# Attention and mixture-of-experts layer: last weight chunks, exponentials and down weights moved between engines around the start of the expert blocks

## The chip, the cores and the metric

One core of a Trainium2 chip runs the whole kernel in a single launch. The metric is the device time of one execution in microseconds; lower is better. Engine names: PE is TensorE's matmul stream, PEld its weight loads, DVE is VectorE, ACT is ScalarE, POOL is GpSimd, SP is SyncE. Where a row has a "q" behind the engine's name, it is the engine's queue, which also issues DMAs.

## What is computed

The input is 16 sequences of 512 rows of 256 numbers. A residual layer of windowed attention with a latent branch comes first, then a residual feed-forward layer with shared weights and 8 experts, of which each row uses 2. The second layer is the part that matters here:

```python
x = x + _layernorm(attention(_layernorm(x)))
x = x + _layernorm(ffn(_layernorm(x)))

# ffn, for every row: E = 8 experts, K = 2 chosen, F = 352, shared F = 704
scores = softmax(x @ gate_w.T)
topk_w, topk_i = top_k(scores, K)
topk_w = topk_w / (topk_w.sum(-1, keepdims=True) + 1e-20) * 2.5
combine = zeros((T, E)).at[arange(T)[:, None], topk_i].set(topk_w)
g = silu(einsum('td,edf->etf', x, w_gate)) * einsum('td,edf->etf', x, w_up)
y = einsum('te,etd->td', combine, einsum('etf,efd->etd', g, w_down))
return y + (silu(x @ sw_gate) * (x @ sw_up)) @ sw_down
```

## The kernel before, in words

The program runs in four parts. The attention of all 16 sequences comes first. In the second part (lines 1968 to 2230) the router chooses the experts of all rows, and the shared feed-forward layer is computed for the first 8 sequences, in 8 steps; `m` counts them from 0 to 7. In the third part (lines 2236 to 2533) the chosen experts work through 135 blocks of 128 rows. In the fourth part the shared layer of the other 8 sequences is computed and everything is summed. There is no loop in hardware: every instruction is written out, each engine works through its own list in order, and semaphores hold the lists together.

Exact products in single precision are made of three matmuls, so every weight and every row is needed as a rounded high part and as a remainder (the raw number minus the high part). The weights of the experts are prepared while the second part runs:

- **Gate and up weights** come in 16 chunks of 128x704 (`expert_chunk`, line 1988). POOL makes the high part and the remainder of each in `split_chunk` (line 2028): a copy at line 2032 and a subtraction at line 2034. Chunks 14 and 15 are split by POOL after all its scatters. Chunk 15 has its own place in `arena`; the others pass through `chunk_in`.
- **Down weights** come as three parts, `n` = 0, 1, 2, of 128, 128 and 96 partitions by 2048. In the third part DVE rounds parts 0 and 1 and forms their remainders (lines 2398 to 2403); ACT rounds part 2 (line 2345) and DVE forms its remainder (line 2408).
- **The list of rows**: POOL scatters the number of every row into `list_scratch` with indirect DMAs (line 2025), 8 for each of two kinds of sequences in each step. In the last step DVE forms the `table` (`finish_table`, line 2101), which says for every block where its names stand and which expert it uses.

In the last step (`m` = 7) of the second part six slices `n` = 0 to 5 of the shared hidden layer pass: PE's `gate_up`, ACT's `gate_silu` (line 534), DVE's `hidden` (line 551), ACT's `hidden_high` (line 540), DVE's `hidden_low` (line 557), PE's `shared_down`. ACT does `first_chunk(n)`, which is `gate_silu` of slice n and then `hidden_high` of slice n. `h_used` counts PE's finished `shared_down`.

At the start of the third part:

- **SP** waits for the table and for the landing of all scatters (`lists_written`), and then loads names in groups (`GROUPS`, line 2236). Group n waits until group n - 3 has landed. The last shared result is stored behind group 2.
- **POOL** waits for `h_used` and then gathers the rows of a block (`gather`, line 2293, DMA at line 2300), which needs the names' group. Six gathers run ahead; then gather b + 6 alternates with scatter b.
- **PE** does 18 matmuls whose result nobody reads (line 2457), then waits for the table, for all chunks and for ACT's reading of the shared result. Then `turn_rows` of blocks 0 and 1 (line 2472), and in step b: `block_gate_up` b (lines 2484 to 2486, 12 matmuls), `turn_rows` b + 2, `turn_hidden` b - 1 (line 2494), `down` b - 2 (lines 2505 to 2507). Before step 2 it waits for the remainders of all three parts of the down weights:

```python
for b in range(NBLK + 2):
    if b == 2:
        pe.wait_ge(down_low, FCE)
```

- **ACT** first makes the exponentials for the router's weights (line 2319) and a small Silu that brings the other function table back (line 2320), rounds part 2 and then works on the blocks (`rows_high` at 2324, `gate` at 2330).
- **DVE** works on the down weights and then on the blocks: `rows_low` (line 2371), `gated_hidden` (line 2376), `hidden_low` (lines 2380 and 2382).

## Time and profile before

| what | value |
|---|---|
| three runs | 1854.68, 1858.62 and 1861.70 us, median 1858.62 |
| the profiled execution's own time | 1857.21 us |
| its span in the profile | 1855.3 us |
| mean granted clock of TensorE over the span | 0.978 of full speed |
| busy share of PE, PEld, DVE, ACT, POOL | 94%, 77%, 68%, 53%, 50% |
| third part (the expert blocks), from the trace | about 1132 to 1632 us |

The span is what lies between the first and the last instruction of the trace; the execution's own time is 1.9 us longer. A row of a timeline gives the start in microseconds from the span's beginning, the duration, the engine and line of the code, what is written and read, and in brackets how long the engine had been idle before and what released it. A row of windows gives, for a stretch A:B, its length, the busy time of each engine asked for, the granted clock of TensorE as a share of its full 2.4 GHz (1.00 is 2.4 GHz, 0.50 is 1.2 GHz), the mean busy share of the DMA engines and the GB/s they moved.

### The profile page before, as it was taken

To read this page: it belongs to the slowest core of one execution; us is meant where nothing else is said; L and a number is where in the kernel's file an instruction comes from. 1 tells how busy PE (TensorE), PEld (TensorE's weight loads), DVE (VectorE), ACT (ScalarE), POOL (GpSimd) and SP (SyncE) were. 2 spreads that over 40 slices of the span, in tenths; PEclk is the share of its full clock that TensorE was granted. 3 is DMA by queue.
4 is the path that set the end of the run, shared out by engine and by line. 5 is a ranking of instruction groups with operands and counts; after the bars stand their busy time and mean duration, and the time that the engine had idled before them with its cause. 6 is when DMAs were issued, how large, how long until landed. Compare 5 with 4: busy or idle time off the path is not lost.

```text
span 1855.3 us, 39544 instructions
## 1 busy us (share of the span) xinstructions
PE 1740.7 (94%) x13060; PEld 1425.3 (77%) x13060; DVE 1259.0 (68%) x3077; ACT 992.1 (53%) x2309; POOL 932.3 (50%) x1117
## 2 busy tenths in 40 slices
PE   4999999999999999997999998999999999989996
PEld 3566666666666666655888887999999999978886
DVE  7778888888888888785776775433333333358787
ACT  2566666777777667666333333444444444435554
POOL 3445555555555555554378766455555555401101
PEclk8999999999999999998999999999999999999999
DMA  6655556655565665443254322233222222257875
GB/s 120 100 74 92 103 102 127 115 98 102 103 101 100 109 115 104 92 91 120 92 113 89 90 42 57 70 76 87 75 75 75 75 75 76 71 191 184 204 210 97
DMA packets 164113, 189.78 MB, mean 102 GB/s; under 512 B 41777, under 2 KB 121970, under 8 KB 163922
## 3 DMA queue, kind: packets, MB, share of 16 engines
q1 hardware_dynamic: 136642, 142.92, 36.9%
q0 software_dynamic: 24976, 43.41, 9.4%
q8 instruction: 116, 1.90, 0.5%
q10 hardware_dynamic: 2304, 0.93, 0.3%
q14 instruction: 75, 0.61, 0.2%
HBM read 84.87 MB, written 51.40 MB: 73 GB/s over the span
## 4 chain that ended last, share of the span: by engine, by line
PE 69%; DVE 8%; ACT 7%; issue 6%; POOL 5%; SPq 3%; DMA 1%; ACTq 1%; POOLq 0%; DVEq 0%
PE bank L496 5%; PE bank L497 5%; PE bank L498 5%; PE bank L1636 5%; PE bank L2485 4%; PE bank L2486 4%; PE bank L2484 4%; PE bank L1693 4%; PE bank L1658 4%; PE bank L1638 3%; ACT prob L1074 3%; PE bank L1637 3%; PE bank L2505 2%; PE bank L2506 2%; PE bank L2507 2%
## 5 line engine op out<-in xcount | busy, mean ns | idle before, releaser
L924 POOL TENSOR_SCALAR_AFFINE_SELECT prob<-prob 128x512 f32<-128x512 f32 x256 | 162.9, 636 | 380.3 <-ACT prob L1074 380.2
L1074 ACT ACTIVATE prob<-bank 128x512 f32<-128x512 f32 (+1 forms) x512 | 249.0, 539 | 103.4 <-PE bank L1680 100.8
L2376 DVE TENSOR_TENSOR b_h<-b_h,bank 128x352 f32<-128x352 f32 x135 | 70.4, 521 | 287.3 <-ACT b_h L2330 287.3
L2306 POOL DMA_INDIRECT y_scratch<-b_y,names x135 | 133.6, 989 | 176.4 <-ACT b_y L2341 172.4
L1399 DVE COPY_PREDICATED bank<-from_prev,bank 128x512 f32<-128x512 int32 x192 | 133.1, 693 | 96.2 <-PE bank L1658 92.0
L1402 DVE TENSOR_REDUCE row_max<-bank 128x4 f32<-128x512 f32 x256 | 177.3, 693 | 25.8 <-PE bank L1658 18.5
L2484 PE MATMUL bank<-wgu_h,bxT_h 128*128 x540 | 176.5, 327 | 0.0
L2485 PE MATMUL bank<-wgu_l,bxT_h 128*128 x540 | 176.2, 326 | 0.0
L2330 ACT ACTIVATE b_h<-bank 128x352 f32<-128x352 f32 x135 | 62.7, 464 | 211.9 <-PE bank L2486 211.9
L2486 PE MATMUL bank<-wgu_h,bxT_l 128*128 x540 | 175.3, 325 | 0.0
L2300 POOL DMA_INDIRECT bx<-xn_scratch,names x135 | 134.6, 997 | 54.6 <-issue 39.2
L1693 PE MATMUL bank<-prob,v_sb 128*32 128x256 f32 (+1 forms) x2048 | 159.4, 366 | 0.0
L2025 POOL DMA_INDIRECT list_scratch<-names,pos x128 | 128.3, 1002 | 46.9 <-issue 36.1
L1658 PEld LDWEIGHTS bank<-kS,qS 48*128 48x128 f32 x1024 | 78.3, 189 | 92.9 <-issue 48.7
L1658 PE MATMUL bank<-kS,qS 48*128 48x256 f32 (+1 forms) x1024 | 127.8, 328 | 20.9 <-DVE row_max L1402 20.8
L928 POOL TENSOR_SCALAR_AFFINE_SELECT prob<-prob 128x512 f32<-128x512 f32 x192 | 128.3, 668 | 0.0
L2505 PE MATMUL bank<-wd_h,bhT_h 128*128 (+1 forms) x405 | 125.5, 310 | 0.7 <-ACT b_y L2341 0.7
L2507 PE MATMUL bank<-wd_h,bhT_l 128*128 (+1 forms) x405 | 114.7, 283 | 0.0
L2506 PE MATMUL bank<-wd_l,bhT_h 128*128 (+1 forms) x405 | 114.2, 282 | 0.0
L2634 POOL DMA_DIRECT2D out_dram<-f_ys x15 | 19.5, 1300 | 186.9 <-ACT f_ys L2656 186.9
L1680 PE MATMUL bank<-qS,kS 49*128 49x256 f32 (+1 forms) x1024 | 106.6, 285 | 5.3 <-ACT prob L1074 4.6
L2485 PEld LDWEIGHTS bank<-wgu_l,bxT_h 128*128 128x128 f32 x540 | 102.7, 190 | 0.0
(359 smaller groups left out, 5247.5 us busy)
## 6 DMA issues: line engine op xcount, KB each, us to landing
kS<-qk_h SPq DMA_DIRECT2D x128, 128.0 KB, 3.9
qS<-qk_h SPq DMA_DIRECT2D x128, 128.0 KB, 5.8
f_y<-y_scratch SPq DMA_DIRECT2D x16, 1024.0 KB, 9.2
x_in<-in_L_attn_x_dram SPq DMA_DIRECT2D x16, 512.0 KB, 6.2
kS<-qk_l SPq DMA_DIRECT2D x64, 128.0 KB, 4.8
qS<-qk_l SPq DMA_DIRECT2D x64, 128.0 KB, 6.6
x_res<-in_L_attn_x_dram SPq DMA_DIRECT2D x16, 512.0 KB, 4.1
out_dram<-x_res SPq DMA_DIRECT2D x16, 512.0 KB, 5.1
```

Of the source, the lines that this page charges most:

```text
L924: op = e.affine_select(out=own, in_=own, compare_op=ALU.is_gt, fill=0.0, base=0, pattern=[[0, HG], [1, P]], channel_multiplier=-1)
L1074: e.activation(prob[:, u % SLOTS, 2 * hp:2 * hp + 2, 0:w], src[:, :, 0:w], ACT.Exp, scale=SCALE).then_inc(keyed.frees[hp], 1)
L1402: e.tensor_reduce(row_max[:, g, :, b], own, AX.X, ALU.max).then_inc(score_free, 1)
L1658: op = e.matmul(SB[:, par, hh * WIN + lo:(hh + 1) * WIN], qS[rows, buf, tile, b * P:(b + 1) * P], kS[rows, buf, tile, k0:k0 + w], start=(b ...
L1693: op = e.matmul(PV[h * PAD:(h + 1) * PAD, b * P:b * P + w], v_sb[:, buf, b, g * HG + h, :], prob[:, u % SLOTS, 2 * (h % 2) + h // 2, 0:w], ...
L2300: e.indirect_dma_start(out=bx[:, b % 4, :], out_offset=None, in_=rows_dram, in_offset=bass.IndirectOffsetOnAxis(ap=b_names[:, b, 0:1], axis=0)
L2484: e.matmul(out_, xh, wh, start=(c == 0), stop=False)
L2485: e.matmul(out_, xh, wl, start=False, stop=False)
L2486: op = e.matmul(out_, xl, wh, start=False, stop=(c == C - 1))
L2505: e.matmul(out_, hh, wh, start=(n == 0), stop=False)
L2506: e.matmul(out_, hh, wl, start=False, stop=False)
L2507: op = e.matmul(out_, hl, wh, start=False, stop=(n == FCE - 1))
```

## The change

Five things are edited, all around the border of the second and the third part.

1. POOL no longer splits chunks 14 and 15. ACT makes their high parts in the last step, after slices 1 and 2, and waits there until chunk 15 has landed. DVE makes the remainders, chunk 14's behind `experts_reached` and chunk 15's behind `hidden_low` of slice 3.
2. The exponentials move on ACT from the start of the third part into the last step, behind slice 3. The small Silu is left out.
3. ACT rounds all three parts of the down weights, part 0 ahead of the copy of the last shared result, parts 1 and 2 behind it. That copy moves from the second part to the third. DVE only forms the remainders: part 0 first, part 1 behind `rows_low` of blocks 0 and 1, part 2 behind its step 0 of the blocks.
4. Names are loaded in groups of 1, 1, 2, 4, 8, 16, 32 and 71 blocks, not 1, 1, 2, 12, 40 and 79.
5. PE's matmuls that nobody reads are 14, not 18. The buffer `b_h` lies behind `bhT_h` and `bhT_l`, not ahead of them, and ACT's wait for the stored shared result moves from `gate` to `hidden_turned`.

```diff
-            ROUTE_STEPS, END_STEPS, WEIGHT_STEPS, LAST_STEPS = 20, 8, 12, 17
+            ROUTE_STEPS, END_STEPS, WEIGHT_STEPS, LAST_STEPS = 20, 8, 10, 17
...
-        b_h = sb("b_h", [P, 2, F])
         bhT_h = sb("bhT_h", [P, 2, FCE, P], f32r)
         bhT_l = sb("bhT_l", [P, 2, FCE, P], f32r)
+        b_h = sb("b_h", [P, 2, F])
...
                     for kind in "ba":
                         scatter(kind, HALF - 1)
-                    for k in (CHUNKS - 2, CHUNKS - 1):
-                        split_chunk(k)
...
+                    def last_chunk_high(k):
+
+                        act.wait_ge(stage_in, 32 * CHUNKS)
+                        act.wait_ge(stage_split, CHUNKS - 2)
+                        nc.scalar.activation(parts_of(k)[0], chunk_of(k), ACT.Copy).then_inc(chunk_high, 1)
+
+                    def exponentials():
+
+                        act.wait_ge(member_ready, 2 * HALF)
+                        nc.scalar.activation(probs, lg_all[:, :, :], ACT.Exp).then_inc(exp_ready, 1)
...
+                            if m == HALF - 1:
+                                if n in (1, 2):
+                                    last_chunk_high(CHUNKS - 3 + n)
+                                if n == 3:
+                                    exponentials()
                         if m + 1 < HALF:
                             gate_silu(act, m + 1, 0, h_f)
-                    result(HALF - 1)
...
+                    def last_chunk_low(k):
+
+                        dve.wait_ge(chunk_high, k + 1)
+                        hi, lo = parts_of(k)
+                        e.tensor_tensor(lo, chunk_of(k), hi.bitcast(f32), ALU.subtract).then_inc(stage_split, 1)
...
                         experts_reached()
+                        last_chunk_low(CHUNKS - 2)
                         hidden(dve, m, 3, h_f)
                         hidden_low(dve, m, 3, h_f, h_h, h_l)
+                        last_chunk_low(CHUNKS - 1)
                         finish_table()
...
-            GROUPS = [range(0, 1), range(1, 2), range(2, 4), range(4, 16), range(16, 56), range(56, NBLK)]
+            GROUPS = [range(0, 1), range(1, 2), range(2, 4), range(4, 8), range(8, 16), range(16, 32), range(32, 64), range(64, NBLK)]
...
-                    act.wait_ge(member_ready, 2 * HALF)
-                    e.activation(probs, lg_all[:, :, :], ACT.Exp)
-                    e.activation(picked[:, 0:1, :], lg_all[:, 0:1, :], ACT.Silu).then_inc(exp_ready, 1)
...
                     act.wait_ge(down_in, 16 * FCE)
+                    act.wait_ge(table_ready, 1)
+                    down_rounded(0)
+                    act.wait_ge(h_used, FCS * HALF)
+                    for n in range(2):
+                        shared_result(act, HALF - 1, n, lambda n: y_sb[:, 2 * n:2 * n + 2, :].rearrange("p t d -> p (t d)"))
+                    act.wait_ge(stage_split, CHUNKS)
+                    down_rounded(1)
                     act.wait_ge(hl_ready, FCS * HALF)
-                    e.activation(wd_h[0:fe[LATE], LATE, :, :], wd_f[0:fe[LATE], LATE, :, :], ACT.Copy).then_inc(down_high, 1)
+                    down_rounded(2)
                     rows_high(0, 0)
                     rows_high(1, 1)
...
-                    dve.wait_ge(down_in, 16 * FCE)
-                    for n in range(LATE):
+                    def down_remainder(n):
+                        dve.wait_ge(down_high, n + 1)
                         hi, lo, raw_ = down_part(n)
-                        if n == 1:
-                            dve.wait_ge(stage_split, CHUNKS)
-                        link(e.tensor_copy(hi, raw_))
                         e.tensor_tensor(lo, raw_, hi.bitcast(f32), ALU.subtract).then_inc(down_low, 1)
+
+                    down_remainder(0)
                     rows_low(0, 0)
                     rows_low(1, 1)
-                    dve.wait_ge(down_high, 1)
-                    hi, lo, raw_ = down_part(LATE)
-                    e.tensor_tensor(lo, raw_, hi.bitcast(f32), ALU.subtract).then_inc(down_low, 1)
+                    down_remainder(1)
...
                         step(b, b % 2)
+                        if b == 0:
+                            down_remainder(2)
...
-                    for _ in range(18):
+                    for _ in range(14):
                         e.matmul(psum[0][:, :], wsd_h[:, 0, 0:P], ws_h[:, 0, 0:4 * P], start=True, stop=True)
```

On ACT, from the Silu of slice 4 of the last step to the first blocks, this stood in a row before (`h_f` and `h_h` are the slices, `rows_a` written from `lg_all` holds the exponentials, `y_sb` the shared result, `wd_h` the rounded down weights, `bxT_h` the turned rows of a block):

```order
L534 ACTIVATE h_f<-bank 128x512
L540 ACTIVATE h_h<-h_f 128x512
L534 ACTIVATE h_f<-bank 64x512
L540 ACTIVATE h_h<-h_f 64x512
L544 ACTIVATE y_sb<-bank 128x512 x2
L2315 UNCONDITIONAL_BRANCH
L2319 ACT_TABLE_LOAD
L2319 ACTIVATE rows_a<-lg_all 128x512
L2320 ACT_TABLE_LOAD
L2320 ACTIVATE rows_a<-lg_all 128x8
L2345 ACTIVATE wd_h<-wd_l 96x2048
L2324 ACTIVATE bxT_h<-bank 128x256 x2
```

With the change ACT's list from the high part of slice 2 on reads:

```order
L540 ACTIVATE h_h<-h_f 128x512
L2071 ACT_TABLE_LOAD
L2071 ACTIVATE rows_a<-lg_all 128x512
L534 ACT_TABLE_LOAD
L534 ACTIVATE h_f<-bank 128x512
L540 ACTIVATE h_h<-h_f 128x512
L534 ACTIVATE h_f<-bank 64x512
L540 ACTIVATE h_h<-h_f 64x512
L2338 UNCONDITIONAL_BRANCH
L2363 ACTIVATE wd_h<-wd_l 128x2048
L544 ACTIVATE y_sb<-bank 128x512 x2
L2363 ACTIVATE wd_h<-wd_l 128x2048
```

The two table loads now stand ahead of `gate_silu` of slice 4, and behind the last slice one rounding stands ahead of the shared result and two behind it.

On DVE, at the start of the third part (`wd_l` is the remainder of the down weights, `b_h` the hidden rows of a block), this stood before:

```order
L2402 CAST wd_h<-wd_l 128x2048
L2403 TENSOR_TENSOR wd_l<-wd_l,wd_h 128x2048
L2402 CAST wd_h<-wd_l 128x2048
L2403 TENSOR_TENSOR wd_l<-wd_l,wd_h 128x2048
L2371 TENSOR_TENSOR bxT_l<-bank,bxT_h 128x256 x2
L2408 TENSOR_TENSOR wd_l<-wd_l,wd_h 96x2048
L2376 TENSOR_TENSOR b_h<-b_h,bank 128x352
L2371 TENSOR_TENSOR bxT_l<-bank,bxT_h 128x256
```

With the change:

```order
L2429 TENSOR_TENSOR wd_l<-wd_l,wd_h 128x2048
L2400 TENSOR_TENSOR bxT_l<-bank,bxT_h 128x256 x2
L2429 TENSOR_TENSOR wd_l<-wd_l,wd_h 128x2048
L2405 TENSOR_TENSOR b_h<-b_h,bank 128x352
L2400 TENSOR_TENSOR bxT_l<-bank,bxT_h 128x256
L2429 TENSOR_TENSOR wd_l<-wd_l,wd_h 96x2048
L2405 TENSOR_TENSOR b_h<-b_h,bank 128x352
```

Both copies are gone from DVE, and the remainders of parts 1 and 2 have moved back behind the first work on blocks.

## Rows read from the trace of the kernel before

**Rows 1.** The page: busy time, share of the span and instructions

```profile
PE 1740.7 (94%) x13060; PEld 1425.3 (77%) x13060; DVE 1259.0 (68%) x3077; ACT 992.1 (53%) x2309; POOL 932.3 (50%) x1117
```

**Rows 2.** Timeline of PE around the border, start, duration, instruction, idle before

```profile
1118.57 0.40 PE L496 MATMUL bank<-rT_h,ws_h 128*128 128x512 f32 x1
...
1132.14 4.27 PE L2457 MATMUL bank<-ws_h,wsd_h 128*128 128x512 f32 x18
1139.55 0.44 PE L2472 MATMUL bank<-ident,bx 128*128 128x128 f32 x2 [3.15 <-DMA bx<-xn_scratch,names]
1142.61 0.69 PE L2472 MATMUL bank<-ident,bx 128*128 128x128 f32 x2 [2.62 <-DMA bx<-xn_scratch,names]
1142.95 0.64 PE L2484 MATMUL bank<-wgu_h,bxT_h 128*128 x1
...
1149.71 0.41 PE L2484 MATMUL bank<-wgu_h,bxT_h 128*128 x1
...
1153.77 0.33 PE L2484 MATMUL bank<-wgu_h,bxT_h 128*128 x1
...
1157.32 0.33 PE L2484 MATMUL bank<-wgu_h,bxT_h 128*128 x1
```

**Rows 3.** The chain of waits, from the last scatter to the first names

```profile
1126.61 4.62 DMA list_scratch<-names,pos
1131.46 2.55 DMA names<-list_scratch
```

**Rows 4.** Timeline of POOL: a scatter of the list, gathers 0, 1 and 4

```profile
1119.74 1.48 POOL L2025 DMA_INDIRECT list_scratch<-names,pos  x1 [0.30 <-issue]
...
1134.81 2.90 POOL L2300 DMA_INDIRECT bx<-xn_scratch,names  x1 [0.50 <-issue]
1138.01 2.73 POOL L2300 DMA_INDIRECT bx<-xn_scratch,names  x1 [0.30 <-issue]
...
1149.08 0.95 POOL L2300 DMA_INDIRECT bx<-xn_scratch,names  x1 [5.84 <-DMA names<-list_scratch]
```

**Rows 5.** Timeline of DVE in the last step and behind it

```profile
1119.68 0.69 DVE L557 TENSOR_TENSOR h_l<-h_f,h_h 128x512 fp32r<-128x512 f32 x1 [0.70 <-ACT h_h L540]
...
1125.79 0.67 DVE L551 TENSOR_TENSOR h_f<-h_f,bank 128x512 f32<-128x512 f32 x1
1127.15 1.76 DVE L557 TENSOR_TENSOR h_l<-h_f,h_h 128x512 fp32r<-128x512 f32 x1 [0.70 <-ACT h_h L540]
...
1132.77 3.68 DVE L2403 TENSOR_TENSOR wd_l<-wd_l,wd_h 128x2048 fp32r<-128x2048 f32 x1
...
1137.62 2.29 DVE L2403 TENSOR_TENSOR wd_l<-wd_l,wd_h 128x2048 fp32r<-128x2048 f32 x1
...
1143.75 0.42 DVE L2371 TENSOR_TENSOR bxT_l<-bank,bxT_h 128x256 fp32r<-128x256 f32 x1 [2.88 <-ACT bxT_h L2324]
```

**Rows 6.** Timeline of SP: the names of blocks 4 to 15

```profile
1134.77 12.69 SPq L2275 DMA_DIRECT2D names<-list_scratch  x12
```

**Rows 7.** Timeline of ACT in the last step and behind it

```profile
1112.40 0.63 ACT L540 ACTIVATE h_h<-h_f 128x512 fp32r<-128x512 f32 x1 [2.67 <-DVE h_f L551]
...
1133.50 1.28 ACT L2319 ACT_TABLE_LOAD   x1
1134.80 0.64 ACT L2319 ACTIVATE rows_a<-lg_all 128x512 f32<-128x512 f32 x1
...
1136.85 1.89 ACT L2345 ACTIVATE wd_h<-wd_l 96x2048 fp32r<-96x2048 f32 x1
```

**Rows 8.** Windows: length, clock, DMA share and GB/s, where chunk 15 has landed

```profile
1114.50:1114.75 0.25, 1.00 0.01 1
```

**Rows 9.** Windows: length, PE busy, clock, DMA share and GB/s

```profile
1143.60:1146.60 3.00, 3.00 (x11) 0.50 0.25 50
...
1147.60:1149.20 1.60, 1.60 (x11) 0.99 0.25 63
```

**Rows 10.** Line 2025: time from issue to landing of all 128 scatters

```profile
DMA to landing us min/median/max: 2.5/4.3/7.4
```

More of the change, by code:

```diff
@@ L1978, in chunk_of, with parts_of @@
                     return chunk_in[:, :] if k < CHUNKS - 1 else arena[:, LAST_CHUNK:LAST_CHUNK + 2 * F]
+                def parts_of(k):
+                    return tuple(w[:, k, :, :].rearrange("p k f -> p (k f)") for w in (wgu_h, wgu_l))
                 def store_result(sp, m):
@@ L2028, in split_chunk @@
                     def split_chunk(k):
-                        hi, lo = (w[:, k, :, :].rearrange("p k f -> p (k f)") for w in (wgu_h, wgu_l))
-                        gp.wait_ge(stage_in, 32 * (CHUNKS if k >= CHUNKS - 2 else k + 1))
+                        hi, lo = parts_of(k)
+                        gp.wait_ge(stage_in, 32 * (k + 1))
                         e.tensor_copy(hi, chunk_of(k)).then_inc(chunk_high, 1)
@@ L2326, in gate @@
                     def gate(b, u):
-                        if isinstance(b, int) and b == 0:
-                            act.wait_ge(ys_stored, 16 * HALF)
                         act.wait_ge(bg_full, b + 1)
@@ L2341, in result, with down_rounded @@
                         e.activation(b_y[:, u, :], psum[5][:, 0:D], ACT.Copy).then_inc(by_read, 1)
+                    def down_rounded(n):
+                        e.activation(wd_h[0:fe[n], n, :, :], wd_f[0:fe[n], n, :, :], ACT.Copy).then_inc(down_high, 1)
                     act.wait_ge(down_in, 16 * FCE)
+                    act.wait_ge(table_ready, 1)
[5 more added lines that the diff above has]
+                    down_rounded(1)
                     act.wait_ge(hl_ready, FCS * HALF)
-                    e.activation(wd_h[0:fe[LATE], LATE, :, :], wd_f[0:fe[LATE], LATE, :, :], ACT.Copy).then_inc(down_high, 1)
+                    down_rounded(2)
                     rows_high(0, 0)
```

4 lines of the change are left out of this document (3 added, 1 removed).

## The prediction

> **What bounds the kernel now.** I read the page first: PE is busy for 94% of the span, no other engine over 77% [rows 1], so time is to be had only where PE stands still or is slow. The change touches nothing but the border between the shared layer and the expert blocks, so I read PE's timeline there. The reader is to see two holes behind the 18 unread matmuls: 3.15 us until the rows of block 0 are there and 2.62 us until those of block 1 are [rows 2]. Then PE is slow: eleven matmuls in 3.00 us at 1143.6 to 1146.6, with a granted clock of 0.50 (1.2 GHz), after PE had been idle for 3.15 us, busy for 0.44 and idle again for 2.62; from 1147.6 on it is eleven in 1.60 at 0.99 [rows 2, 9]. From block 2 to block 3 PE needs 4.06 us (1149.71 to 1153.77), from 3 to 4 it needs 3.55 (to 1157.32) [rows 2]. After that the blocks follow at 3.55 us, and nothing in the change alters that pace. So the question is how much earlier block 3 begins.
>
> What holds the rows back is a chain [rows 3, 4]: the last scatter is issued at 1126.61 and lands 4.62 us later, SP issues the first names at 1131.46, they land 2.55 us later at 1134.0, and POOL gathers. POOL was busy with chunk 15 until 1134.31 and begins at 1134.81, only 0.8 us late. But its two gathers take 2.90 and 2.73 us, where the later one takes 0.95 [rows 4]. PE's two turns start 1.84 and 1.87 us after these gathers' ends.
>
> Why were they slow? DVE's subtraction of 2.29 us starts at 1137.62 and ends at 1139.91; gather 1, begun inside it at 1138.01, ends 0.83 us after that [rows 4, 5]. The scatter begun at 1119.74, inside a DVE subtraction that ends at 1120.37, takes 1.48 us and ends 0.85 after it [rows 4, 5]. And DVE's subtraction begun at 1132.77, while POOL subtracts for chunk 15 until 1134.31, takes 3.68 us, not 2.29 [rows 5]: POOL and DVE hold each other up while both read this memory.
>
> **Part by part.**
>
> *Chunks 14 and 15 leave POOL.* POOL is free from 1127.6. It gains the 0.8 us until the names' landing, no more, as SP's chain is not shortened. `hidden_low` of slice 4, which took 1.76 us beside POOL's work, takes 0.69 [rows 5]; that brings PE's end of the shared layer from 1132.14 to about 1131.1, ahead of the names, so it is worth nothing by itself.
>
> *ACT takes the high parts.* ACT is free at 1113.03 [rows 7], but chunk 15 lands only at about 1114.5, where the DMA share falls to 0.01 [rows 8]: a wait of 1.5 us. Behind it in ACT's queue stands `gate_silu` of slice 2. The copy of 704 numbers I put at 0.79 us, between 0.63 for 512 and 1.89 for 2048 [rows 7]. Slice 2's Silu (0.6) then ends at 1115.9 and DVE has read the banks at 1116.6, some 1.3 us later than before. PE asks for these banks again at 1118.57, for slice 4 [rows 2]. Cost on the path: zero, as long as chunk 15 lands before about 1116.4.
>
> *DVE takes the remainders.* Each is 0.89 us by the rate of 0.69 for 512 and 2.29 for 2048 [rows 5]. DVE had idle time before the table, so these cost DVE nothing on the path. They can cost POOL: the scatters start every 1.27 us, and one that starts inside a remainder waits. Bounds: zero if both fall between starts, 2 x 0.89 = 1.8 us if both hit at once. The one hit of 0.5 us before [rows 4] moves as well. I reckon starts against my shifted DVE times and find one hit and the old one gone or shifted: 0.3 us later names.
>
> *The exponentials.* Two table loads of 1.28 us and 0.64 us of work [rows 7] now stand ahead of slice 4's Silu. ACT had the high part of slice 3 at 1119.68 [rows 5]; the late slice 2 (1.3) and chunk 14's remainder (0.89) make that at most 1121.9, and 1121.5 by my reckoning, as DVE was idle for 0.3 in between. So Silu ends at 1121.5 + 1.28 + 0.64 + 1.28 + 0.6 = 1125.3. DVE wants it behind the table, at 1125.79 [rows 5]: hidden, with 0.5 us to spare. The rows show no pause around a load: it begins at 1133.50 and the exponential starts at 1134.80, 1.30 us later [rows 7]. The Trainium skill ("ScalarE: Activation LUTs", What ACT_TABLE_LOAD costs) speaks against this step: it counts a drain of about 1380 ns beside each load's 1283. This trace does not show it. By that page Silu would end 2.8 us later, 2.2 after DVE wants it, and the whole gain below would fall from 4.9 to 3.7 us, as an estimate; I go by the rows.
>
> *Down weights.* ACT had slice 5's high part at 1130.3 (DVE's 0.69 us and PE's last eight matmuls lie between it and 1132.14), and has it 1.1 earlier now, at 1129.2. It rounds part 0 in 1.89 us [rows 7] to 1131.1, copies the shared result to 1132.4 and rounds two parts to 1136.2. It is wanted for block 0's rows at 1137.6, so this is hidden by 1.4 us. DVE's remainder of part 0 then lies at 1131.1 to 1133.4, over before the first gather. That is the core of the gain: gathers 0 and 1 meet no DVE subtraction. The Trainium skill ("SBUF — State Buffer", Who interferes with whom) says that a VectorE instruction with two inputs in this memory and a GpSimd instruction that reads it shut each other out for a whole instruction. The trace agrees for those begun inside (0.83 and 0.85 us after the end). By that rule the remainders of parts 1 and 2 would hold gathers 4 and 5, which I find harmless below.
>
> *Start of the blocks, by the rows.* Names land at 1134.0 + 0.3 = 1134.3. Gather 0 runs to 1135.3 (0.95 us), gather 1 starts 0.30 us later and ends at 1136.55. PE turns block 1 at + 1.87 = 1138.4 and starts block 0's matmuls 0.34 later [rows 2], at 1138.8: **4.2 us** before 1142.95. The clock: PE's unread matmuls now end at about 1131.1 + 14 x 0.237 = 1134.4, then 2.7 us idle and 0.9 us idle. Before, idle of 3.15 and 2.6 brought it down; I take full clock, since the second hole is short. Block 0's twelve matmuls then take 2.0 us. DVE's low part of block 1 comes 1.14 us after PE's turn [rows 2, 5], at 1139.55 to 1139.9; the remainder of part 1 runs until 1142.2, the hidden rows of block 0 (0.45) and the low part of block 2 (0.35) until 1143.0, and part 2's remainder until 1145.3. PE would be ready for block 2 at 1143.7, but waits for that remainder: a **new stall of 1.6 us**. Block 2 starts at 1145.35, 4.36 us before 1149.71 [rows 2].
>
> *Names in growing groups.* Gather 4 waited 5.84 us for twelve names that SP issued at 1.06 us each [rows 4, 6]. Four names now need 4.2 us and land at about 1140.8; gathers 4 and 5, even held up to the ends of both remainders, land at 1145 and 1148.5, ahead of PE's need at 1147.4 and 1151. Later groups stay ahead: SP issues a name in 1.06 us, a block lasts 3.55. So block 3 follows in 3.55 us, not 4.06: **0.5 us**. Buffer places and moved waits: nothing.
>
> **Sum:** 4.2 + 0.16 + 0.5 = 4.9 us. Against the profiled execution's 1857.21 us that is 1852.3; the median of the runs shown is 1.4 us above that execution, and against it the sum gives **1853.7 us**.
>
> **The bounds.** Clock low in block 0: its matmuls take 3.5 us, but most hides in the new stall, and 0.5 is lost; low through block 2 as well, 2.0 more. Scatters hit: between + 0.3 and - 1.5. No stall at block 2: + 1.6. The last scatter's landing: 4.62 us here, but 2.5 at least and 7.4 at most over all [rows 10], so + 2.1 or - 2.8. ACT and DVE copies at half speed beside others: see below.
>
> **The rivals.**
> - *Larger gain.* POOL's splitting delayed the last landing, and it falls towards 2.5 us: names 2.1 us earlier, 1858.6 - 7.0 = **1851.6**. For it: POOL worked on chunks just then. Against: the median landing is 4.3 anyway.
> - *The gain comes back at block 2.* DVE's remainders of parts 1 and 2 take 3.68 us each, as beside POOL before [rows 5]. Block 2 starts 2.8 us later than above, leaving 2.1: **1856.5**. For it: gathers 4 and 5 run just then. Against: a gather is short, the subtraction that took 3.68 met POOL's own long one.
> - *The table loads cost more than the rows show,* or the change moves a wait rather than removing it: slice 4 is 2.2 us late, part 0's remainder runs until 1135.6 and holds gather 0 by 1.15: **1854.9**.
> - *Slower than before.* If ACT's first rounding is late enough that part 0's remainder lies over gathers 0 and 1, they take 2.90 and 2.73 us again, block 0 starts at 1142.95 as before, and now two remainders of up to 3.68 us stand between block 1's low part and block 2, where before part 2's alone stood: 1144.1 + 3.7 + 0.4 + 0.4 + 3.7 = 1152.3, 2.6 us after 1149.71; less the 0.5 of the names: **1860.7**. It decides from the point where ACT ends the rounding of part 0 more than 1.0 us later than I reckon. For it: DVE has no slack at block 2. Against: ACT's row of 1.89 us has no contention in it.
>
> **How the numbers follow.** Forecast 58%, larger gain 14%, given back at block 2 12%, table loads 8%, slower 8%. About 0.5%, or 9.3 us, is what a measurement of this kernel can tell from no change. None of the cases reaches that by itself: faster by more needs every favourable bound together (2.1 + 1.6 on top of 4.9) and a favourable median, 9%; slower by more 4%; within it 87%. The three runs shown lie 3.9 us below to 3.1 above their median, so the range is 1848.5 to 1859.5; it holds all cases but the slowest, with the spread of a median.
>
> **What would show it.** Right: gathers 0 and 1 under 1.1 us; block 0's first matmul near 1138.8 and block 3's near 1148.9; PE waiting 1 to 2 us at block 2 for DVE's remainder; ACT idle about 1.5 us ahead of the first chunk copy; Silu of slice 4 done before 1125.8. Wrong: long gathers again, a first turn later than 1139, PE waiting for slices in the last step, a clock of 0.50 beyond block 1, or a difference that lies outside 1110 to 1160 us.

## The result, and the profile after

The changed kernel runs in 1849.26 us in the median of 14 runs (1841.80 to 1853.67); the kernel before, timed beside it, in 1858.01 us (1850.71 to 1865.91, 14 runs). The ratio is 0.995, with an interval from 0.9935 to 0.9965: 8.75 us faster by the medians, where 4.9 were forecast. The time lies in the range of the prediction, 0.8 us above its lower end, but the gain is 1.8 times the sum. The profiled execution took 1851.47 us.

The page of the changed kernel, span and busy times:

```profile
span 1849.7 us, 39539 instructions
PE 1739.9 (94%) x13056; PEld 1424.9 (77%) x13056; DVE 1252.8 (68%) x3077; ACT 996.1 (54%) x2312; POOL 926.4 (50%) x1113
```

The span is 5.6 us shorter than before [rows 1]. It has to be divided, because this execution was slower in a part that the change does not touch. ACT's first table load of the second part, before and after:

```profile
875.08 1.28 ACT L534 ACT_TABLE_LOAD   x1
```

```profile
877.13 1.28 ACT L534 ACT_TABLE_LOAD   x1
```

And POOL's first scatter of the last 16, before and after:

```profile
1106.90 0.97 POOL L2025 DMA_INDIRECT list_scratch<-names,pos  x1 [2.22 <-DVE pos L700]
```

```profile
1110.53 0.96 POOL L2028 DMA_INDIRECT list_scratch<-names,pos  x1 [2.22 <-DVE pos L700]
```

The changed kernel came 3.63 us later to this scatter, from where both do the same work. From there to the end of the span it gained 5.6 + 3.6 = 9.2 us. In the fourteen profiles of this study the table load begins anywhere from 869.0 to 877.1 us, though no instruction ahead of it differs. These 8.1 us are two thirds of the 11.9 us over which the changed kernel's 14 runs spread. So for every kernel I use a **stretch** that this does not touch: from the first of the last 16 scatters to the start of ACT's Silu of block 20. It is 114.38 us before (1106.90 to 1221.28) and 105.28 us after (1110.53 to 1215.81): 9.10 us, which agrees with the 8.75 of the medians. Behind it nothing differs: 634.0 us to the end of the span before, 633.9 after.

Every stretch is read from one execution, and it holds some chance as well. In ten kernels gather 0 waits for nothing but its names and still begins at places up to 0.66 us apart: 26.96 us behind the first scatter in `e4_dve_rounds`, 27.62 in `e12_all_three`; in an eleventh, `e6_unread25`, at 28.52. So a difference of less than about 0.7 us between two stretches is not shown by the stretches alone, and I say where gather 0 began when it matters.

Times behind the first scatter are written with a plus: before, block 0's first matmul starts at +36.05. PE around the border, after, answering to [rows 2]:

```profile
1134.68 3.36 PE L2485 MATMUL bank<-ws_h,wsd_h 128*128 128x512 f32 x14
1140.88 0.44 PE L2500 MATMUL bank<-ident,bx 128*128 128x128 f32 x2 [2.83 <-DMA bx<-xn_scratch,names]
1142.00 0.44 PE L2500 MATMUL bank<-ident,bx 128*128 128x128 f32 x2 [0.69 <-DMA bx<-xn_scratch,names]
1142.35 0.42 PE L2512 MATMUL bank<-wgu_h,bxT_h 128*128 x1
...
1149.62 0.42 PE L2512 MATMUL bank<-wgu_h,bxT_h 128*128 x1 [0.80 <-DVE wd_l L2429]
...
1153.27 0.33 PE L2512 MATMUL bank<-wgu_h,bxT_h 128*128 x1
```

Block 0 starts at +31.82, 4.2 us earlier than before; block 2 at +39.09, behind a new wait of 0.80 us for DVE's remainder; block 3 at +42.74, 4.1 us earlier. POOL and DVE, after, answering to [rows 4, 5]:

```profile
1137.90 1.00 POOL L2323 DMA_INDIRECT bx<-xn_scratch,names  x1 [6.59 <-DMA names<-list_scratch]
1139.20 0.96 POOL L2323 DMA_INDIRECT bx<-xn_scratch,names  x1 [0.30 <-issue]
...
1143.85 2.50 POOL L2323 DMA_INDIRECT bx<-xn_scratch,names  x1 [1.17 <-DMA names<-list_scratch]
```

```profile
1134.83 2.29 DVE L2429 TENSOR_TENSOR wd_l<-wd_l,wd_h 128x2048 fp32r<-128x2048 f32 x1 [1.25 <-ACT wd_h L2363]
...
1143.24 2.28 DVE L2429 TENSOR_TENSOR wd_l<-wd_l,wd_h 128x2048 fp32r<-128x2048 f32 x1
...
1147.18 2.28 DVE L2429 TENSOR_TENSOR wd_l<-wd_l,wd_h 96x2048 fp32r<-96x2048 f32 x1
```

The first two gathers take 1.00 and 0.96 us, not 2.90 and 2.73. Gather 4, begun inside the remainder of part 1 (1143.24 to 1145.52), takes 2.50 us and ends 0.83 us behind it; nobody waits for it. ACT in the last step, after, answering to [rows 7]:

```profile
1118.48 0.79 ACT L2066 ACTIVATE wgu_h<-chunk_in 128x704 fp32r<-128x704 f32 x1 [1.82 <-DMA arena<-in_L_ffn_w_up_dram]
...
1125.14 1.28 ACT L2071 ACT_TABLE_LOAD   x1
1126.43 0.63 ACT L2071 ACTIVATE rows_a<-lg_all 128x512 f32<-128x512 f32 x1
1127.09 1.28 ACT L534 ACT_TABLE_LOAD   x1
1128.38 0.60 ACT L534 ACTIVATE h_f<-bank 128x512 f32<-128x512 f32 x1
```

And a window inside block 0's matmuls: length, PE busy, clock, DMA share and GB/s. The clock is down, as in [rows 9]:

```profile
1142.80:1145.80 3.00, 3.00 (x12) 0.50 0.69 212
```

That leaves 9.1 - 4.1 = 5.0 us. My sum ended at block 5. ACT's Silu of blocks 14 and 15, before:

```profile
1194.98 0.46 ACT L2330 ACTIVATE b_h<-bank 128x352 f32<-128x352 f32 x1 [1.55 <-PE bank L2486]
...
1203.53 0.46 ACT L2330 ACTIVATE b_h<-bank 128x352 f32<-128x352 f32 x1 [2.23 <-PE bank L2486]
```

After, the same two:

```profile
1194.49 0.46 ACT L2347 ACTIVATE b_h<-bank 128x352 f32<-128x352 f32 x1 [1.55 <-PE bank L2514]
...
1198.04 0.46 ACT L2347 ACTIVATE b_h<-bank 128x352 f32<-128x352 f32 x1 [1.55 <-PE bank L2514]
```

Between these blocks 8.55 us passed before, and 3.55 do now. What stopped it before, on POOL and then on PE:

```profile
1195.38 0.97 POOL L2300 DMA_INDIRECT bx<-xn_scratch,names  x1 [7.79 <-DMA names<-list_scratch]
```

```profile
1198.18 0.44 PE L2472 MATMUL bank<-ident,bx 128*128 128x128 f32 x2 [3.24 <-DMA bx<-xn_scratch,names]
```

POOL stood 7.79 us with gather 16 waiting for names, and PE 3.24 us for these rows. The other 1.8 us are the clock, for the most part: it was 0.64 in the 3 us from 1198 on and 0.79 in the 3 us behind them, about 1.6 us of lost time by the busy time of PE there (2.81 x 0.36 + 3.00 x 0.21, an estimate). The list of what ended the idle time ahead of POOL's gathers (line 2300) had it in one row:

```profile
  DMA names<-list_scratch: 13.6, 2
```

Two waits, 13.6 us in all. I had accounted for one of 5.84.

### The profile page after: what moved, and what is told of

It is laid out like the page before. It is cut to its first block, busy times and chain, and to the rows that moved or that the text cites. A ratio compares the mean times of both kernels' runs of the same rounds, so it can differ in the third digit from the quotient of the medians.

```text
span 1849.7 us, 39539 instructions
## 1 busy us (share of the span) xinstructions
PE 1739.9 (94%) x13056; PEld 1424.9 (77%) x13056; DVE 1252.8 (68%) x3077; ACT 996.1 (54%) x2312; POOL 926.4 (50%) x1113
## 4 chain that ended last, share of the span: by engine, by line
PE 72%; DVE 8%; ACT 7%; issue 6%; POOL 5%; DMA 1%; ACTq 1%; SPq 0%; POOLq 0%; DVEq 0%
PE bank L496 5%; PE bank L497 5%; PE bank L498 5%; PE bank L1636 5%; PE bank L2514 5%; PE bank L2512 5%; PE bank L2513 5%; PE bank L1693 4%; PE bank L1658 4%; PE bank L1638 4%; PE bank L1637 4%; ACT prob L1074 3%; PE bank L2533 3%; PE bank L2534 3%; PE bank L2535 3%
## 5 line engine op out<-in xcount | busy, mean ns | idle before, releaser
L2512 PEld LDWEIGHTS bank<-wgu_h,bxT_h 128*128 128x128 f32 x540 | 101.9, 189 | 1.2 <-issue 1.1
```

What stands on the lines that cost most here:

```text
L2512: e.matmul(out_, xh, wh, start=(c == 0), stop=False)
```

## The experiments

My theory A after the result: more than half of the gain is the growing groups. The old group of 40 names, issued by SP at 1.06 us each, landed too late for block 16. The rival, theory B, is my prediction's own split: 0.5 us for the groups, the rest from work moved between engines.

### Groups alone, and everything but the groups

`e1_groups_only`, on the kernel before:

```diff
-            GROUPS = [range(0, 1), range(1, 2), range(2, 4), range(4, 16), range(16, 56), range(56, NBLK)]
+            GROUPS = [range(0, 1), range(1, 2), range(2, 4), range(4, 8), range(8, 16), range(16, 32), range(32, 64), range(64, NBLK)]
```

> The kernel before with one edit: the names are loaded in groups of 1, 1, 2, 4, 8, 16, 32, 71. Measure: the stretch from the first of the last 16 scatters of the list to ACT's Silu of block 20, 114.4 us before and 105.3 us with the whole change. Theory A (the growing groups bring more than half of the gain, because block 16 no longer waits for a group of 40 names, where blocks 15 and 16 lay 8.55 us apart and not 3.55): both pauses go, 5.0 + 0.4 us, so the stretch is 109.0 us and the time about 1852.5 us. Theory B (the groups are worth the 0.5 us at block 4 that I predicted, and the rest came from the work moved between engines): 113.9 us and 1857.5 us.

Measured: stretch 109.51 us, median 1854.04 us against 1857.08 beside it (ratio 0.9991, 0.9971 to 1.001). The gap of 8.55 us is 3.55. Theory A had 109.0 and B 113.9: A holds. The timed runs alone would not show it: their interval holds no change as well as 4.9 us, and its middle is 1.7 us. The trace does, by a pause of 5.0 us that is gone. All of the gain lies there; block 3's Silu comes at +49.10, where it came at +49.00 before. The gathers stayed long:

```profile
1135.14 3.25 POOL L2300 DMA_INDIRECT bx<-xn_scratch,names  x1 [0.15 <-issue]
1138.70 2.73 POOL L2300 DMA_INDIRECT bx<-xn_scratch,names  x1 [0.30 <-issue]
```

`e2_all_but_groups`, on the changed kernel, is the same diff the other way round.

> The changed kernel with one edit undone: groups of 1, 1, 2, 12, 40, 79 again. Same stretch (114.4 before, 105.3 with the whole change). Theory A: the names of block 16 land when SP has issued 40 of them, at 1.06 us each, from a start that the change moves by only 0.1 us; what the blocks start earlier is given back at block 16: 114.2 us, blocks 15 and 16 some 12 to 13 us apart (8.55 plus the 4 us of earlier start), and a time of about 1858 us. Theory B (the parts add up): the 3.7 us that the start is earlier stay: 110.3 us, about 1854 us.

Measured: stretch 112.27 us, median 1855.06 us (ratio 1.0, 0.9986 to 1.0014). It lies between the two theories, 2.1 us better than before, 7.0 worse than the changed kernel. Block 0 starts at +31.74, as early as in the changed kernel. Then POOL and ACT show:

```profile
1143.91 0.95 POOL L2323 DMA_INDIRECT bx<-xn_scratch,names  x1 [10.32 <-DMA names<-list_scratch]
```

```profile
1142.98 0.46 ACT L2347 ACTIVATE b_h<-bank 128x352 f32<-128x352 f32 x1 [2.40 <-PE bank L2514]
...
1152.31 0.47 ACT L2347 ACTIVATE b_h<-bank 128x352 f32<-128x352 f32 x1 [2.19 <-PE bank L2514]
```

Gather 4 begins at +42.18, as in the kernel before (+42.18 there too), since the names of its group land no earlier. So the early start is given back at block 3 (9.33 us behind block 2, not 3.55), and more than that: PE stands still for 4.02 us, the clock falls behind it (0.67 from 1149 to 1152), and block 3's Silu comes at +50.58, 1.6 us later than in the kernel before. The 2.1 us are therefore not what is left of the early start. They arise at block 16, where the gap is 4.85 us and not 8.55: the blocks come 1.6 us later and the names 0.6 us earlier (gather 16 at +87.91, not +88.48), PE waits 1.08 us and not 3.24, and the clock stays at 1.00 behind so short a wait, where it was 0.64 before. I had put the place of the loss at block 16; the mechanism is the one of theory A, the place is the first group that is too large. The parts do not add: the groups are worth 4.9 us without the rest and 7.0 us with it, the rest 2.1 us without the groups and 4.2 with them.

### POOL's splitting and DVE's rounding

`e3_pool_splits`, on the changed kernel (ACT's and DVE's parts for the two chunks taken out):

```diff
                     for kind in "ba":
                         scatter(kind, HALF - 1)
+                    for k in (CHUNKS - 2, CHUNKS - 1):
+                        split_chunk(k)
...
-                                if n in (1, 2):
-                                    last_chunk_high(CHUNKS - 3 + n)
...
-                        last_chunk_low(CHUNKS - 2)
...
-                        last_chunk_low(CHUNKS - 1)
```

> The changed kernel, but POOL splits chunks 14 and 15 after its scatters as before, and ACT and DVE do nothing for them in the last step. Same stretch. Theory A (POOL and DVE shut each other out): DVE's remainder of part 0 is held until POOL's last subtraction ends, then holds gather 0 until 0.83 us after its own end; both gathers end 2.0 us later than in the changed kernel, stretch 107.4 us. Rival (POOL's splitting was hidden behind the landing of the names but for 0.5 us): gathers 0 and 1 take 0.97 us each and the stretch is 105.8 us.

Measured: stretch 106.01 us, median 1850.09 us (ratio 0.9965, 0.9943 to 0.9987). It is nearer to the rival. Gather 0 and DVE's first remainder:

```profile
1131.97 2.28 POOL L2321 DMA_INDIRECT bx<-xn_scratch,names  x1 [0.75 <-DMA names<-list_scratch]
```

```profile
1130.04 3.33 DVE L2428 TENSOR_TENSOR wd_l<-wd_l,wd_h 128x2048 fp32r<-128x2048 f32 x1 [1.24 <-ACT wd_h L2361]
```

The chain of theory A is there: DVE's remainder takes 3.33 us beside POOL, and gather 0 takes 2.28 us and ends 0.88 us behind it. But it costs 1.2 us and not 2.0, and gather 1 takes 0.95. Part of it goes into the wait at block 2, which is 0.43 us here and not 0.80, and 0.7 us are left.

`e4_dve_rounds`, on the changed kernel:

```diff
-                    act.wait_ge(table_ready, 1)
-                    down_rounded(0)
...
-                    act.wait_ge(stage_split, CHUNKS)
-                    down_rounded(1)
...
+                            link(e.tensor_copy(hi, raw_))
...
                     down_remainder(0)
+                    down_remainder(1)
                     rows_low(0, 0)
                     rows_low(1, 1)
-                    down_remainder(1)
+                    down_remainder(2)
...
-                        if b == 0:
-                            down_remainder(2)
```

> The changed kernel, but DVE rounds parts 0 and 1 of the down weights itself again and forms their remainders right away; ACT rounds part 2 and DVE forms its remainder behind the low parts of blocks 0 and 1. Same stretch. Theory A: DVE is busy on these four until about 2.8 us after the first names have landed, gather 0 takes about 3.5 us, gather 1 0.97; block 0 starts 2.5 us later than in the changed kernel, the pause of 0.8 us at block 2 goes: stretch 107.0 us. Rival (the long gathers came from POOL's own state after the splitting, not from DVE): both gathers 0.97 us, no pause at block 2, stretch 104.5 us.

Measured: stretch 105.17 us, median 1848.53 us (ratio 0.9962, 0.9945 to 0.9979): no loss that can be told. Its names came early by chance (gather 0 at +26.96, where it is +27.37 in the changed kernel), so up to 0.3 us of loss may be hidden. POOL's first two gathers:

```profile
1132.18 1.67 POOL L2323 DMA_INDIRECT bx<-xn_scratch,names  x1 [6.18 <-DMA names<-list_scratch]
1134.15 1.98 POOL L2323 DMA_INDIRECT bx<-xn_scratch,names  x1 [0.30 <-issue]
```

They are 1.67 and 1.98 us long, so DVE holds them, which the rival denies; block 0 starts 1.3 us later. Theory A's mechanism holds and its 2.5 us do not: without POOL beside it, DVE does its first copy and remainder in 1.23 and 2.29 us, not 1.68 and 3.68. And what block 0 loses comes back at block 2, where no remainder is waited for. So undoing one of the two costs 0.7 or -0.1 us, both about as small as chance, and yet `e1_groups_only`, which has both undone, is 4.2 us longer than the changed kernel.

`e9_pool_and_dve` undoes both in the changed kernel (the two diffs above together).

> The changed kernel with both undone: POOL splits chunks 14 and 15 after its scatters, and DVE rounds parts 0 and 1 of the down weights. The exponentials stay in the last step, there are 14 unread matmuls, and the growing groups stay. One of the two undone gave 106.0 and 105.2 us where the changed kernel has 105.3. Theory A (the two only cost together: POOL's last subtraction holds DVE's first, and so DVE's row of four lies over both gathers): gathers 0 and 1 about 2.9 and 2.7 us, stretch 109 us. Rival (each part has its own price, so they add; the 4.2 us that the groups alone leave come from the exponentials or from 18 unread matmuls): 105.9 us and gather 1 at 0.96 us.

Measured: stretch 109.70 us, time 1851.20 us in one execution. POOL's gathers and DVE's first remainder:

```profile
1132.12 3.10 POOL L2321 DMA_INDIRECT bx<-xn_scratch,names  x1 [0.30 <-issue]
1135.53 2.73 POOL L2321 DMA_INDIRECT bx<-xn_scratch,names  x1 [0.31 <-issue]
```

```profile
1130.28 3.69 DVE L2431 TENSOR_TENSOR wd_l<-wd_l,wd_h 128x2048 fp32r<-128x2048 f32 x1
```

Neither undone 105.28, one 106.01, the other 105.17, both 109.70: the price lies in the pair. POOL's splitting holds DVE three times: `hidden_low` of slice 4 takes 1.77 us where it takes 0.69 in `e4_dve_rounds`, the first copy 1.68 and not 1.23, the first remainder 3.69 and not 2.29. These 2.9 us make the row of four on DVE end late enough to lie over both gathers (3.10 and 2.73 us). Either edit breaks it: from 109.70 us, one alone brings 3.7 us (to 106.01) and the other alone 4.5 (to 105.17). As this kernel has the exponentials in the last step, 14 unread matmuls and the new place of `b_h` with the moved wait, and is as slow as `e1_groups_only` to within 0.2 us, those make up nothing of the 4.2 us that can be told.

### The exponentials

`e5_exp_back`, on the changed kernel:

```diff
-                                if n == 3:
-                                    exponentials()
...
+                    act.wait_ge(member_ready, 2 * HALF)
+                    e.activation(probs, lg_all[:, :, :], ACT.Exp)
+                    e.activation(picked[:, 0:1, :], lg_all[:, 0:1, :], ACT.Silu).then_inc(exp_ready, 1)
                     act.wait_ge(down_in, 16 * FCE)
                     act.wait_ge(table_ready, 1)
                     down_rounded(0)
```

> The changed kernel, but the exponentials and the small Silu stand at the start of the third part again, ahead of ACT's rounding of part 0. Stretch from the first of the last 16 scatters to the Silu of block 20: 105.3 us in the changed kernel. Theory A (ACT's queue is what feeds DVE there): 3.4 us ahead of the rounding push DVE's remainder of part 0 over gather 1, which then ends 0.8 us after it, block 0 starts 1.6 us later and, as part of that is given back in the pause at block 2, the stretch is 106.3 us. Rival (ACT has slack, the step is worth nothing): 105.3 us. If the Silu of slice 4 had been late in the changed kernel, this one would have a shorter last step; by its trace it was not.

Measured: stretch 106.62 us, time 1848.20 us in one execution. Theory A (106.3 us), with gather 1 at 1.94 us, ending 0.83 us behind the remainder; block 0 starts 1.2 us later, where 1.6 were expected. Having the exponentials early (and 14 unread matmuls, not 18) is worth nothing that can be told before ACT has the roundings (`e9_pool_and_dve` against `e1_groups_only`: 109.70 and 109.51). Once ACT has them, the early exponentials are worth 1.3 us: they make room for the roundings.

### The clock, and the wait at block 2

`e6_unread25`, on the changed kernel:

```diff
-                    for _ in range(14):
+                    for _ in range(25):
```

> The changed kernel with 25 unread matmuls, not 14, so that PE is busy until the rows of block 0 have nearly landed. Theory A (the clock falls because PE stands still for 2.8 us before block 0): the clock stays at 1.00, block 0's Silu comes 1.4 us earlier, but DVE's remainder of part 2 now decides when block 2 starts, so only half is kept: stretch 104.5 us, pause at block 2 about 1.6 us and not 0.8. Rival (the clock falls for another reason, as it did with 18 and with 14): block 0 as slow as before and 105.3 us.

Measured: stretch 105.46 us, time 1852.85 us in one execution. The clock stayed up: from block 0's first matmul to its Silu 2.24 us pass, not 3.56. But SP's first four names took 3.45 us to issue here, not 1.91, and gather 0 began 1.15 us later. Why is open. And PE waited 1.33 us for DVE's remainder at block 2, not 0.80 (1.6 expected). The late names and that longer wait cancel what the clock gave, so the run shows the clock's part and not its worth.

`e7_early_round`, on the changed kernel:

```diff
                             if m == HALF - 1:
+                                if n == 1:
+                                    act.wait_ge(down_in, 16 * FCE)
+                                    nc.scalar.activation(wd_h[:, 0, :, :], wd_f[:, 0, :, :], ACT.Copy).then_inc(down_high, 1)
...
-                    down_rounded(0)
+                    act.wait_ge(stage_split, CHUNKS)
+                    down_rounded(1)
                     act.wait_ge(h_used, FCS * HALF)
...
-                    act.wait_ge(stage_split, CHUNKS)
-                    down_rounded(1)
...
                     down_remainder(0)
+                    down_remainder(1)
                     rows_low(0, 0)
                     rows_low(1, 1)
-                    down_remainder(1)
+                    down_remainder(2)
...
-                        if b == 0:
-                            down_remainder(2)
```

> The changed kernel, but ACT rounds part 0 of the down weights in the last step while it waits for chunk 15, and part 1 at the start of the third part; DVE forms both remainders there in a row, and part 2's behind the low parts of blocks 0 and 1. Theory A (part 2's remainder is what block 2 waits for): the pause of 0.8 us at block 2 goes, gather 0 is held by about 0.1 us, block 0 starts as in the changed kernel: stretch 104.2 us. Rival (DVE's second remainder runs into the gathers and costs what it saves): gather 0 over 2 us and a stretch of 105.3 us or more.

Measured: stretch 104.18 us, median 1849.07 us (ratio 0.9965, 0.9946 to 0.9985). Theory A (104.2), closer than one execution can show: no wait at block 2, gather 0 at 1.17 us, block 0 at +31.80. The 1.1 us can be seen in the stretch alone; the timed runs do not tell this kernel from the changed one.

`e8_early_round_unread25` has both edits.

> Both edits of the two kernels before: early rounding of part 0 and 25 unread matmuls. Theory A: with the pause at block 2 gone the higher clock is kept whole, so the parts together bring more than their sum: stretch 102.7 us, about 2.6 us less than the changed kernel and 11.7 less than before, a time of about 1845.5 us where before has 1857. Rival (the parts only add: 0.8 and 1.1): 103.4 us.

Measured: stretch 103.44 us, the shortest of the study, median 1845.82 us (ratio 0.9942, 0.9922 to 0.9962). Gather 0 began at +27.00, 0.37 us earlier than in the changed kernel, so that much of it may be chance. That is the rival's number, but not by its reason: the clock is up (2.24 us to the Silu), but PE turned blocks 0 and 1 together, at +31.13, 0.8 us later than in `e7_early_round`:

```profile
1138.95 0.89 PE L2501 MATMUL bank<-ident,bx 128*128 128x128 f32 x4 [1.13 <-DMA bx<-xn_scratch,names]
```

Three more kernels went after that. `e10_early_round_unread21` has `range(21)`:

> Early rounding of part 0, and 21 unread matmuls. With 25, the turns of blocks 0 and 1 started together at 31.1 us behind the first scatter, 0.8 us later than with 14, and block 0 lost part of what the clock gave. Theory A (25 are so many that PE or its memory reads come in the way of block 0's first turn; 21 end 1 us earlier): turn at 30.3 us, clock at 1.00, stretch 102.6 us. Rival (the late turn had another cause, such as the stored shared result whose 512 KB are under way when the first rows are gathered): turn at 31 us again in this kernel, stretch 103.4 us.

Measured: stretch 104.43 us, longer than either theory has it, median 1847.13 us (ratio 0.9949, 0.9932 to 0.9967). The first turn starts at +30.58, 1.85 us behind the end of gather 0, with the store where it was; so the store does not explain the late turn in `e8_early_round_unread25` (2.69 us behind). Nor do 25 unread matmuls by themselves: `e6_unread25` has both, and its first turn starts 2.04 us behind the end of gather 0. The cause is open. The clock stays up, but a new wait appears: gather 4 began inside DVE's remainder, took 2.82 us, and PE waited for it:

```profile
1142.77 0.44 PE L2501 MATMUL bank<-ident,bx 128*128 128x128 f32 x2 [1.18 <-DMA bx<-xn_scratch,names]
```

`e11_store_later`, on `e10_early_round_unread21`:

```diff
-                        if n == 2:
-                            store_result(sp, HALF - 1)
                         if n == 3:
+                            store_result(sp, HALF - 1)
```

> The kernel with early rounding and 21 unread matmuls, and SP stores the last shared result behind the names of blocks 4 to 7, not ahead of them, so that no large transfer is under way when the rows of blocks 0 and 1 are gathered. If the store delays the first rows, PE's turn of block 0 starts 1.85 us behind the end of gather 0 and the stretch is 102.5 us, whatever the kernel without this edit does. Rival (the store costs nothing there): the same stretch as that kernel; if ACT's wait for the store then comes late, block 0's turned hidden rows wait and the stretch is longer by up to 1 us.

Measured: stretch 104.16 us, median 1848.03 us (ratio 0.9952, 0.9933 to 0.997). The first turn starts at +30.26, 1.83 us behind the end of gather 0, as in the kernel without this edit (1.85): the rival holds, the store costs nothing there. Gather 4 begins ahead of DVE's remainder (1142.89 against 1142.98) and takes 0.95 us. But the clock fell in block 0. Two windows inside block 0's matmuls, first of `e10_early_round_unread21`, then of this kernel:

```profile
1137.00:1139.00 2.00, 2.00 (x13) 1.00 0.58 148
```

```profile
1141.80:1144.80 3.00, 3.00 (x13) 0.62 0.95 290
```

`e12_all_three` is `e11_store_later` with `range(25)`:

> Early rounding of part 0, the store behind the names of blocks 4 to 7, and 25 unread matmuls. With 21 and the late store the clock fell in block 0 although PE had been idle for only 1.17 and 0.91 us ahead of it, with 21 and the early store it stayed up after 1.20 and 0.87 us, but gather 4 was held by DVE's remainder and PE waited 1.2 us for it. Theory A (with more unread matmuls the idle time ahead of the first turn is short enough, and with the late store gather 4 begins ahead of DVE's remainder and takes 0.95 us): clock at 1.00 in block 0, no pause up to block 20, stretch 102.7 us. Rival (whether the clock falls is not set by these holes alone): block 0 slow again and 104.2 us.

Measured: stretch 103.91 us, between theory A and its rival, median 1847.16 us (ratio 0.9948, 0.9929 to 0.9967). The clock stayed up, as in theory A. But SP's first names were late by 0.5 us behind the first scatter (+24.91, not +24.44), gather 4 fell into DVE's remainder again and took 2.75 us, and PE waited for it:

```profile
1143.95 0.44 PE L2500 MATMUL bank<-ident,bx 128*128 128x128 f32 x2 [0.63 <-DMA bx<-xn_scratch,names]
```

All stretches and ratios (ratio to the kernel before, timed beside each):

| kernel | stretch us | ratio | interval |
|---|---|---|---|
| before | 114.38 | | |
| everything but the groups | 112.27 | 1.0 | 0.9986 to 1.0014 |
| POOL splits, DVE rounds | 109.70 | | |
| groups alone | 109.51 | 0.9991 | 0.9971 to 1.001 |
| exponentials back | 106.62 | | |
| POOL splits | 106.01 | 0.9965 | 0.9943 to 0.9987 |
| 25 unread | 105.46 | | |
| the change | 105.28 | 0.995 | 0.9935 to 0.9965 |
| DVE rounds | 105.17 | 0.9962 | 0.9945 to 0.9979 |
| early rounding, 21 unread | 104.43 | 0.9949 | 0.9932 to 0.9967 |
| early rounding | 104.18 | 0.9965 | 0.9946 to 0.9985 |
| the same, 21 unread, later store | 104.16 | 0.9952 | 0.9933 to 0.997 |
| the same, 25 unread, later store | 103.91 | 0.9948 | 0.9929 to 0.9967 |
| early rounding, 25 unread | 103.44 | 0.9942 | 0.9922 to 0.9962 |

The kernels without a ratio were timed in one execution. No version beats the change by more than its interval. Early rounding with 25 unread matmuls has the lowest median and the shortest stretch.

## Why the prediction was right and where it failed

**The range was met by luck.** The time of 1849.26 us lies in a range of 11 us whose width came from the rivals and from the spread of three runs. The sum gave 1853.7, and 5.0 of the 9.1 us of gain lie where nothing was forecast. One of the prediction's own signs of being wrong came true: a difference outside 1110 to 1160 us, the one at blocks 14 to 16.

**Start of the blocks: right.** Names were forecast 0.3 us later behind the scatters, they came 0.1 earlier (+24.44, not +24.56). Shifted by 3.63 us, gather 0 was forecast at 1134.3 and began at 1134.27; block 0's first matmul at 1138.8 came at 1138.72; ACT waited 1.82 us for chunk 15 (forecast 1.5); the Silu of slice 4 ended at 1125.35, forecast 1125.3, with 0.44 us to spare.

**The clock: wrong, hidden.** I took full clock for block 0. It fell to 0.50 after idle times of 2.83 and 0.69 us. Block 0 took 3.56 us to its Silu, not about 2.2, and the wait at block 2 was 0.80 us and not 1.6. The text had priced that at 0.5 us; block 2 started at 1145.99, not 1145.35, which is 0.64.

**Sum up to block 3: 4.1 us** where the text had 4.9, the difference being the clock and 0.1 us.

**Names in growing groups: the step that failed.** I priced it at 0.5 us, for gather 4 alone. It measures 4.9 us alone and 7.0 us on top of the rest, in the stretch. "Later groups stay ahead" was worked out for the new groups and never asked of the old ones. The rates stood in the text, and the trace had the start: 40 names at 1.06 us are 42.4 us from 1148.70, where SP began them, so they land at about 1193 or later, and gather 16 was due at about 1187.9 by the pace of 3.55. That is the 7.79 us of waiting and a hole of 3.24 us on PE. The sentence "the blocks follow at 3.55 us, and nothing in the change alters that pace" was false for one block in 135, and that one was worth more than all that I had summed.

**Why the gathers were slow: right in the mechanism, wrong in the credit.** Every slow gather above lies over a DVE instruction. But that ACT rounds for DVE is not "the core of the gain": without it the stretch is 105.17. Taking POOL's splitting and DVE's rounding away removes 4.4 us once, and either does nearly all of it.

**The rule on table loads: not borne out.** "ScalarE: Activation LUTs" (What ACT_TABLE_LOAD costs) of the Trainium skill would have put Silu 2.8 us later, by its drain of about 1380 ns beside each load. After the exponential (1126.43 + 0.63 = 1127.06) the load begins at 1127.09 and the Silu at 1128.38, 1.29 us later. Both loads cost 1.28 us here.

**The rivals.** None happened as written. The one that came nearest is the larger gain, for another reason: the landing of the last scatter took 4.41 us where it took 4.62, not 2.5. DVE's remainders took 2.28 us each, so nothing was given back through them.

## What to carry to other kernels

When a transfer is waited for as a group, compare for every group the time at which its last member is issued with the time at which its first member is due, in the kernel before as in the one after; the first group is not the one that hurts. Price a pair of edits as a pair where one contended resource runs through both: with the other in place each of two cures was worth at most 0.7 us here, and both together 4.4. And a start that is made earlier stays earlier only up to the next thing that is paced by something else; here that was SP's issue of names: with the old groups the stretch was 7.0 us longer, and block 3 came later than before the change although block 0 came 4.3 us earlier.

## What the runs showed of the hardware that I had not expected

An indirect DMA that POOL begins inside a DVE subtraction with two inputs in this memory ends 0.82 to 0.88 us behind it: gather 4 after the change 0.83, gather 5 of `e11_store_later` 0.82, gather 0 of `e3_pool_splits` 0.88. Where a DVE copy follows the subtraction at once, it ends 0.12 us behind the copy: gather 0 of the kernel before at 1137.71 (the copy ran from 1136.37 to 1137.59), of `e9_pool_and_dve` at 1135.22 (1133.89 to 1135.10), of `e1_groups_only` at 1138.39 (1137.06 to 1138.27). So such a gather is held twice.

A subtraction that starts when the gather is already under way does not hold it. Gather 4 of `e11_store_later` began at 1142.89, 0.09 us ahead of the subtraction, and took 0.95 us. Gather 0 of `e4_dve_rounds`, begun inside a copy that ended at 1132.97, ended 0.88 us behind that copy, at 1133.85, in the middle of the subtraction from 1133.01 to 1135.30. My reading, which no run isolates, is that the start of a gather is held by both kinds of DVE instruction and its later part by the copy alone.

The Trainium skill ("SBUF — State Buffer", A bandwidth-pool intuition that's wrong) has about 115 ns behind the end of a DVE copy for a DMA issued by GpSimd; the three rows with 0.12 us agree, the gather that began inside a copy (0.88) does not. The same page (Who interferes with whom) lets a VectorE instruction with two inputs in this memory contend with a GpSimd instruction that reads it, and says that a probe showed `tensor_tensor` not stalling a DMA. Here the first holds at a gather's start (0.82 to 0.88 us behind the subtraction), and the second for a gather that is under way.

Whether TensorE's clock falls is not settled by the lengths of the two holes ahead of block 0 alone: with 1.20 and 0.87 us of idle time it was 1.00 in block 0, with 1.17 and 0.91 us it was 0.62 in a window of it. SP's first four names took 1.91 us to issue in eleven kernels and 3.45 in one. Neither cause was found.
